# A hand-written slot order for a gated attention and feed-forward block: values with keys, queries and outputs in other places, and output rows carried over the slot's end

## The reference

```
def reference(x, ctx, g_xattn, g_ffn, Wq, Wkv, Wout, w_gate_up, w_down):
    q = layernorm(x) @ Wq.T                       # 16 heads of 32
    k, v = split(ctx @ Wkv.T)
    s = where(causal, q_h @ k_h.T / sqrt(32), lowest)
    o = softmax(s) @ v_h                          # per head, then joined
    x = x + tanh(g_xattn) * (o @ Wout.T)
    xq = quant(layernorm(x)); w1 = quant(w_gate_up)
    gate, up = split(xq @ w1.T)                   # 1408 each
    h = quant(silu(gate) * up)
    return x + tanh(g_ffn) * (h @ quant(w_down).T)
```

## Time and profile before

| | us |
|---|---|
| median of 3 runs (lowest, highest) | 743.07 (741.93, 746.26) |
| the profiled execution's own time | 743.81 |
| its span, first to last instruction | 742.0 |
| mean granted clock of PE, of full speed | 0.989 |
| PE, DVE, POOL, ACT busy | 705.7, 608.5, 570.9, 418.4 |

### The profile page before, as it was taken

One profiled execution on the slowest core, in us unless ns is written; L12 is line 12 of the kernel. 1 busy time (PEld: TensorE's weight loads), 2 busy tenths in 40 slices (PEclk: granted clock), 3 DMA queues, 4 the chain that ended last, 5 costly groups with the idle time before them and its releaser, 6 DMA issues.

```text
span 742.0 us, 17026 instructions
## 1 busy us (share of the span) xinstructions
PE 705.7 (95%) x5335; PEld 510.3 (69%) x5360; DVE 608.5 (82%) x1900; ACT 418.4 (56%) x658; POOL 570.9 (77%) x763
## 2 busy tenths in 40 slices
PE   3979999999999999999999998999999999999995
PEld 2868888889878888888888886565444444444442
DVE  5576878888888887787788887769999999999994
ACT  5457658668567567577576565265444344343441
POOL 6438768787787787787787877469888988888883
PEclk9989999999999999999999999999999999999998
DMA  8795977877886887877778759934566675565656
GB/s 250 186 247 158 253 159 220 238 178 210 219 209 192 231 199 210 208 212 211 190 217 226 189 139 236 271 102 121 87 163 143 145 165 132 144 154 129 159 124 193
DMA packets 137983, 137.59 MB, mean 185 GB/s; under 512 B 90381, under 2 KB 99879, under 8 KB 137767
## 3 DMA queue, kind: packets, MB, share of 16 engines
q1 hardware_dynamic: 136832, 135.97, 72.4%
q10 hardware_dynamic: 1063, 0.54, 0.4%
HBM read 40.24 MB, written 25.31 MB: 88 GB/s over the span
## 4 chain that ended last, share of the span: by engine, by line
PE 86%; DVE 4%; SPq 3%; DMA 3%; issue 2%; ACT 2%; POOL 1%; ACTq 1%; DVEq 0%; POOLq 0%
PE psum L2036 19%; PE psum L1642 12%; PE psum L1666 11%; PE psum L1708 10%; PE psum L2046 9%; PE psum L1595 5%; PE psum L1682 5%; PE psum L1654 3%; PE psum L1593 3%; PE psum L1629 3%; SPq L271 2%; PE psum L1684 2%; PE psum L1579 2%; DVE hmax L1503 1%; DMA heads<-nmT 1%
## 5 line engine op out<-in xcount | busy, mean ns | idle before, releaser
L1226 DVE CUSTOM_DVE_ANT_0 junk<-psum,mask 128x128 f32<-128x128 f32 (+1 forms) x512 | 152.3, 353 | 42.2 <-PE psum L1595 41.6
L2036 PE MATMUL psum<-w1q,xqb 128*128 128x512 bf16 (+1 forms) x753 | 158.3, 363 | 1.1 <-issue 0.3
L615 POOL TENSOR_SCALAR_AFFINE_SELECT prob<-prob 128x512 f32<-128x512 f32 x128 | 85.3, 666 | 71.1 <-ACT prob L924 69.7
L924 ACT ACTIVATE prob<-psum 128x768 f32<-128x768 f32 x128 | 103.7, 810 | 60.9 <-PE psum L1684 58.8
L798 POOL TENSOR_TENSOR hidden<-hidden 128x512 f32<-128x512 f32 (+1 forms) x94 | 110.8, 1194 | 29.4 <-ACT hidden L1141 29.3
L2036 PEld LDWEIGHTS psum<-w1q,xqb 128*128 128x128 bf16 x768 | 74.3, 98 | 80.2 <-issue 3.0
L1146 ACT ACTIVATE hidden<-hidden,round_bias,hinv 128x1408 f32<-128x1408 f32 x31 | 48.4, 1560 | 103.4 <-DVE hinv L1513 103.4
L623 POOL TENSOR_TENSOR prob<-prob 128x256 f32<-128x256 f32 x128 | 94.3, 743 | 6.2
L2046 PE MATMUL psum<-w2q,hqT 128*128 128x512 bf16 x331 | 79.0, 386 | 6.0 <-DMA hqT<-hq 5.4
L1642 PE MATMUL psum<-xT_hi,wq_hi 128*128 128x256 f32 x256 | 75.7, 296 | 0.5 <-POOL xT_lo L630 0.4
L1595 PE MATMUL psum<-heads 96*128 96x256 f32 x256 | 75.1, 335 | 0.0
(11 more groups left out here) (127 smaller groups left out, 1780.7 us busy)
## 6 DMA issues: line engine op xcount, KB each, us to landing
heads<-k_hi SPq DMA_DIRECT2D x128, 128.0 KB, 3.9
heads<-q_hi SPq DMA_DIRECT2D x128, 128.0 KB, 4.2
xln<-x_dram SPq DMA_DIRECT2D x16, 512.0 KB, 4.6
heads<-k_lo SPq DMA_DIRECT2D x64, 128.0 KB, 4.3
heads<-q_lo SPq DMA_DIRECT2D x64, 128.0 KB, 2.8
x<-x_dram SPq DMA_DIRECT2D x16, 512.0 KB, 4.6
x_scratch<-x SPq DMA_DIRECT2D x16, 512.0 KB, 4.8
x1b<-x_scratch SPq DMA_DIRECT2D x32, 256.0 KB, 3.4
```

What stands on the lines that cost most here:

```text
L615: pool.affine_select(out=blk, in_=blk, compare_op=ALU.is_ge, fill=0.0, base=0, pattern=[[0, 4], [1, P]], channel_multiplier=-1).then_inc(s ...
L924: act.activation(prob[:, g % 2, pair % 2, 0:CAUSAL // P].rearrange("p k h q -> p h k q"), psum[:, 2:4, 0:CAUSAL].rearrange("p h (k q) -> p ...
L1226: dve.tensor_tensor_reduce(junk[:, n % 2, 0:w], psum[:, h % 2, cols], m, 1.0, LOWEST, ALU.add, ALU.max, mx[:, X % 2, t, h:h + 1]).then_inc ...
L2036: last = pe.matmul(psum[:, bank, 0:w], xqb[:, t % 4, k, :], w1q[:, k, half * I + o:half * I + o + w], start=(k == 0), stop=(k == KH - 1))
```

## The change

All five engines' lists are written in another order, in the slots, the opening and the ending. The calls are the same but for `spare`, 12 matmuls where there were 15, and a few waits that belong to the order. In a slot of PE:

- `values(b+1, 0)` and `values(b+1, 1)` stand together early in the slot; before, the first was done a slot ahead.
- the four `queries` of batch b+2 stand in one slot, between the `keys` and to the end; before, the first two were done a slot ahead.
- `transposed(b+3, 0)` stands at the end and its second tile at the start of the next slot.
- `output(b-1, ...)`: three of four calls close the slot, and `output(b-2, 1, 1)` opens the next.

The core of the diff (SP's, DVE's and PE's slots; POOL's, ACT's, the opening and the ending are rewritten in the same manner):

```
-        WORK = [("V", 1, 1, 6), ("Q", 1, 2, 6), ("K", 0, 2, 7), ("K", 1, 2, 6), ("O", 0, -1, 7), ("T", 0, 3, 6),
+        WORK = [("T", 1, 2, 6), ("V", 0, 1, 6), ("V", 1, 1, 7), ("Q", 0, 2, 6), ("K", 0, 2, 7), ("K", 1, 2, 7),
...
                 def slot(b):                 # SP
-                    spread_k_lo(b + 1, 2)
+                    load_rows(b + 3)
+                    spread_q_lo(b + 1, 2)
                     spread_k_lo(b + 1, 3)
+                    spread_k_hi(b + 1, 2)
+                    move_weights(b + 1)
+                    spread_k_hi(b + 1, 3)
+                    store_xq(b - 3)
+                    load_weights(b + 2)
+                    spread_q_hi(b + 1, 2)
                     store_x1(b - 2)
...
+                    load_residual(b - 1)
...
+                    spread_q_hi(b + 2, 0)
...
                 def opening():               # DVE
-                    ones(0)
                     measure_x(0)
+                    ones(1)
...
+                    low_weights(2, wo_hi, wo_lo, wo_raw)
+                    ones(0)
+                    maxima(0, 0)
...
                 def opening():               # ACT
...
                     copy_k(0, 0)
+                    weights(0)
                     copy_k(0, 1)
...
                 def ending():                # PE
...
                     pe.wait_ge(s["v_copied"], 2 * (B - 1) + 2)
                     output(B - 3, 1, 0)
-                    weigh(B - 2, 3)
+                    score_pair(B - 1, 0)
                     output(B - 3, 1, 1)
-                    pe.wait_ge(s["u_copied"], GROUPS * (B - 2) + 4)
-                    gate_up(0, 0, 0, 4)
...
                 def values(X, t):
-                        if X == 0:
-                            pe.wait_ge(s["split"], 1)
```

More of the change, by code:

```diff
@@ L1381, in ending @@
                     normalise(B - 3, 1)
-                    for h in range(0, 5):
+                    for h in range(0, 3):
+                        maxima(B - 1, h)
+                    residual(B - 4, 1)
+                    for h in range(3, 7):
                         maxima(B - 1, h)
                     low_o(B - 3, 0)
-                    for h in range(5, 10):
+                    for h in range(7, 11):
                         maxima(B - 1, h)
-                    low_o(B - 3, 1)
-                    maxima(B - 1, 10)
@@ L1389, in ending @@
-                    maxima(B - 1, 11)
-                    step(B - 4, 0)
-                    for h in range(12, 16):
+                    measure(B - 4, 0)
+                    for h in range(11, 16):
                         maxima(B - 1, h)
                     negate(B - 1)
+                    measure(B - 4, 1)
+                    low_o(B - 3, 1)
+                    step(B - 4, 0)
+                    reciprocals(B - 2)
+                    split_reciprocals(B - 2)
                     step(B - 4, 1)
+                    normalise(B - 2, 0)
@@ L1768, in opening @@
                     scores(0, 15)
[L1769 to L1771 removed]
                     pe.wait_ge(s["t_copied"], 6)
                     values(1, 0)
[L1774 to L1775 removed]
+                    maxima_rows(0)
+                    pe.wait_ge(s["t_copied"], 5)
+                    values(1, 1)
                     scores(1, 0)
@@ L1837, in slot @@
                     score_pair(b, 2)
-                    keys(b + 2, 0)
+                    queries(b + 2, 0)
                     scores(b + 1, 4)
@@ L1862, in slot @@
                     score_pair(b, 7)
-                    output(b - 1, 1, 0)
-                    maxima_rows(b + 1)
-                    output(b - 1, 1, 1)
-                    weigh(b, 2)
-                    queries(b + 3, 0)
-                    weigh(b, 3)
-                    values(b + 2, 0)
-                    queries(b + 3, 1)
+                    queries(b + 2, 3)
+                    maxima_rows(b + 1)
+                    weigh(b, 2)
+                    output(b - 1, 0, 0)
+                    transposed(b + 3, 0)
+                    weigh(b, 3)
+                    output(b - 1, 0, 1)
+                    output(b - 1, 1, 0)
                 def ending():
```

719 lines of the change are left out of this document (346 added, 373 removed).

## The result

| | before | changed |
|---|---|---|
| median (lowest, highest), us | 743.05 (741.93, 746.26) | 774.70 (772.33, 788.97) |
| ratio, 95% interval | | 1.041 (1.038 to 1.044) |
| span of the profiled execution, us | 742.0 | 774.1 |
| mean granted clock | 0.989 | 0.977 |

It is 4.1% slower; 739.0 had been forecast. The highest of the four changed runs, 788.97, had a lower granted clock (0.961) than the other three and is left out of the ratio. The windows of the changed kernel, which answer to the earlier trace rows: the twelve full slots 1 to 12 (first pair of batch 1 to first pair of batch 13), everything behind them, and three stretches at the halved clock.

What follows compares the result with a forecast made beforehand. PE was taken as the bound, the only engine full in the slots. Slots -2.6, opening -3.0 and ending +1.5 sum to -4.1, giving 739.0 us against the median of 743.07; range 733.5 to 748.

Steps and rivals of the forecast that it cites:

- The queue, taken as no wait: SP's queue ahead of scores(b+1, 8): third quarter's high part of the queries lands 0.4 us before it is wanted.
- The bound of 5.2: Upper end of the 2.3 to 5.2 us taken for the landing of the third quarter's last piece.
- the burst of 2.5 MB within 8 us: Load on SP's queue in a slot, named as the argument for the rival that queries wait there.
- the rule that the prediction cited: Each DMA engine consumes descriptors in ring order, so the third quarter lands behind the rows and weights issued ahead of it.
- The rival of the queue wait: Queries wait on SP's queue at scores(b+1, 8), 0.65 us a slot, at most 1.3; time 747.4; chance 0.2.
- DVE at the slot's end: Inverted sums and residual ready 8.7 and 9.4 us behind the last score, margins 1.1 and 0.9: no wait on PE.
- The joints, -0.2 a slot: Fewer gaps between PE's calls shorten each slot to 28.5 us, -2.6 us over 13 slots, bounds 0 and -5.
- The opening, -3: Up to slot 1's start: earlier key pieces -1, less POOL work -2; -3 us in all, from -5 to +1.5.
- like-for-like start: Slot 1's start before the change, 81.50, set to 77.4 for the calls that leave the opening.
- the two costs named against the gain: Opening: ACT's weights piece ahead of a copy; DVE's low part of Wo (2.3) and memset (3.5) ahead of the first maximum.
- The ending, +1.5: Batch 15's first pair waits longer for its maxima and a w1 load comes later: +1.5 us, from -2 to +5.
- Its mark: Sign for the ending term: the first pair of batch 15 with more than 2 us of waiting.

Runs made afterwards that it cites:

- Experiments 2: Changed kernel with the third quarter's high part of the queries issued two places earlier on SP, ahead of the xq store and weights load: 757.4 us, ratio 1.019.
- experiment 3: Changed kernel, order kept, each w1 piece load in slots 2 to 12 bringing 16 of 128 rows (output wrong): 763.4 us, ratio 1.027.
- experiment 9: On top of 6, the next batch's query high parts go ahead of the keys' low parts on SP: 747.7 us, ratio 1.0052.
- experiment 1: Changed kernel with the third quarter's high part of the queries issued first in SP's slot, ahead of the rows' load: 759.4 us, ratio 1.021.
- 5: On top of experiment 1, maxima_rows(b+1) moved behind weigh(b, 2) on PE: 759.3 us, ratio 1.019.
- 6: On top of experiment 1, POOL's low_k(b+2, 1) moved behind the last mask and sum of the slot: 752.9 us, ratio 1.011.
- 7: Changed kernel with POOL's low_k(b+2, 1) moved behind the slot's last mask and sum, SP's order kept: 784.2 us, ratio 1.051.
- experiment 11: Kernel before with one POOL call moved: the seventh pair's sum ahead of the low part of the second tile's transposed rows: 752.2 us, ratio 1.012.
- experiment 10: On top of experiment 9, low part of Wo and one memset put back behind batch 0's maxima on DVE: 752.0 us, ratio 1.011.
- experiment 4: On top of experiment 1, batch 0's queries issued ahead of rows 2, context 2 and weights 1 in SP's opening: 760.7 us, ratio 1.024.

## Why the prediction was wrong

**The queue, taken as no wait.** This is the step that failed: "With 4.1 for the landing (the burst is long, but 3.5 is the median) and 1.1 for the store it is 11.3, 0.4 before it is wanted. I take no wait." Measured in slot 5: the piece lands 13.1 behind the load's issue, where 11 or so had been said. SP took the 7.0 that the forecast's terms give for it; all of the error is the landing, 6.1 for 4.1 (5.8 on average). The bound of 5.2 was no bound but one slot's highest; the same view of the kernel before, from 111 to 425 us, has 6.0:

```profile
DMA to landing us min/median/max: 2.2/4.0/6.0
```

The forecast had the number in hand ("the burst of 2.5 MB within 8 us") and did not divide it. From the load to the third quarter 2560 KB are issued; at the 208 GB/s of the earlier trace rows they need 12.6 us, against the 11.2 that PE gave them behind the load's issue (211.36 to 222.57, where the scores would start without a wait). That would have said 1.4 us of wait, in every slot. That it comes so close is in part luck. The 208 is a mean over a slot in which the DMA engines are busy for 0.79 of the time; in the burst itself they move more:

```profile
211.36:224.45 13.09, 11.38 (x98) 10.04 (x96) 10.55 (x45) 7.70 (x13) 11.90 (x19) 1.00 0.91 271
```

At 271 GB/s 2560 KB need 9.7 us, and no wait would have been said. But 13.09 us at 271 GB/s are 3.5 MB: some 0.9 MB that are issued behind the piece (a store of 512 KB is the next, 0.6 us later) were moved before it landed. In the twelve slots it was 3.1 to 3.5 MB at 248 to 271 GB/s. So the landing was made of the bytes ahead and of a share of those behind. Experiments 2 and 3 show that bytes decide: at an unchanged place 448 KB less land it 1.8 us earlier in slot 5 and 2.5 on average.

On the rule that the prediction cited: the Trainium skill, page "DMA: Bandwidth & Descriptors", section "Queues, rings and completion order", also says that completion is not in the order of issue. This trace agrees with both halves: the third quarter landed late behind the backlog ahead of it, yet its second piece landed at 224.44, behind the first piece of the fourth quarter, which was issued 1.3 later and landed at 224.16.

**The rival of the queue wait** named the place, the mechanism and the sign, and had a chance of 0.2. Its price, 0.65 a slot and at most 1.3, was three times too small: 1.95 a slot (23.4 in twelve). And it left out the clock: three waits halved it, another 7.4 us.

**DVE at the slot's end.** The forecast took the negation at 0.4 from the kernel before and concluded "Margins of 1.1 and 0.9: no wait" for the inverted sums. These margins held: no wait for `rec` in slots 2 to 12. But the maxima's rows, which wait for the negation, got no margin at all in the working, though the order gave them only a pair and a query call of cover. The change put POOL's low part of keys on top of the negation. In the changed kernel PE's longer wait hid this; it would have cost 1.07 a slot by itself. The Trainium skill, page "SBUF — State Buffer", section "SBUF: two separate sides", names two kinds of DVE instruction that exclude GpSimd: those with two SBUF inputs, against a GpSimd instruction that reads SBUF, and those in a two-port mode. The prediction applied the first kind alone, and in the opening alone. Here the one-input negation was held like the two-input one (0.90 and 0.56 for 0.18 and 0.19); in which mode it ran, no trace shows.

**The joints, -0.2 a slot.** In experiment 9 nine of slots 2 to 12 are 28.68 long, from broadcast to broadcast, against 28.70 before: the term is a tenth of what was said. (The mean of the eleven is 28.70, since two of them are 28.84 and 28.76.) 0.05 to 0.09 a joint was read from single gaps, and the new order's transposes (0.53) and maxima's rows (0.31 for 0.14) have larger ones that were not counted.

**The opening, -3.** The like-for-like start was 77.4. Eight profiles have the changed kernel's opening, call for call. Their starts of slot 1, and how long the clock had been halved until then:

| | changed | 1 | 2 | 3 | 5 | 6 | 7 | 9 |
|---|---|---|---|---|---|---|---|---|
| slot 1 starts | 80.9 | 80.0 | 76.6 | 82.0 | 77.9 | 79.0 | 81.2 | 77.3 |
| halved for, us | 17.1 | 20.5 | 6.8 | 20.5 | 13.7 | 17.1 | 20.5 | 6.8 |

The mean is 79.4, so the opening lost 2.0 where it was to gain 3. With the clock halved as long as before (6.8 us), it is 0.1 to 0.8 ahead. The start goes with the time at the halved clock, which differs between executions of one opening by 14 us; no term of the sum spoke of it, and which wait makes it fall I have not taken apart. That the clock is the cause is not shown either: the old opening stood at 81.5 after 6.8 us of it, and in experiment 11 at 81.8 after 13.7. Of the two costs named against the gain and not priced, experiment 10 says that DVE's order is none; ACT's, a piece of weights ahead of a copy, no run tests. SP's order for the queries of batch 0 is cleared by experiment 4. One more difference is in the traces and not tested: the first negation of batch 0 takes 1.07 us beside POOL in the changed kernel (at 52.22), 0.56 before (at 45.97).

**Slot 1**, in no term, takes 31.3 in experiment 9, where 28.7 less its absent output call would be 27.2. The broadcast stands ahead of everything else and waits 1.1 for the inverted sums; in a steady slot two output calls, 2.9 us, stand between the last weighing and it, in the opening none. The remaining 3 us, a clock halved from 81.2 to 84.6 and pairs that wait for ACT, I have read and not tested.

**The ending, +1.5.** Its mark, more than 2 us of waiting, came in kind and not in size: the first pair of batch 15 waits for the maxima, by this row, and PE loses 1.8 (3.2 had been said).

```profile
512.18 0.39 PE L1676 MATMUL psum<-heads 98*128 98x256 f32 x1 [1.63 <-DMA heads<-nmT]
```

As a whole the sign is the other: from slot 13 on, the same eight profiles take 318.4 on average; before and experiment 11 take 314.4, and 5.6 us of calls have moved in (two query calls 2.9, values 0.8, transposes 0.4, an output 1.5). That is 1.6 gained, within the spread of either group (316 to 321, 313 to 316), and so not shown.

## What to carry to other kernels

When transfers are moved behind others, sum the bytes from the head of the burst to the piece that is waited for, and some of what is issued right behind it (here 2.6 MB, and 0.5 to 0.9 more), and divide by the rate within a burst (here 248 to 271 GB/s), not by the mean of a slot; the highest landing time of one quiet slot is not a bound. A wait that is found is not all there is: give every wait of the new order a margin, for removing one here showed the next three times over, and a fix of the lower one alone gave nothing. Follow POOL's list against DVE's short instructions that PE waits for: the place of one call on POOL was worth 1% of this kernel.

## What the runs showed of the hardware

- A DVE instruction that takes 0.18 us took up to 1.10 while POOL ran an instruction on SBUF, and ended within 0.05 us of POOL's; the two-input one of 0.19 took 0.56. In experiment 1 this happened in slots 2 to 12 without exception; maxima read from PSUM kept their 0.42 in the same stretches.
- The landing of a 128 KB piece was 2.3 us on an empty queue (changed kernel, 227.05) and 6.1 behind 2.3 MB; in experiment 3 448 KB less were worth 1.8 us at an unchanged place in slot 5, and 2.5 on average. Transfers issued behind a piece moved before it had landed: 3.5 MB from the load to the landing in slot 5, of which 2.6 are the pieces up to it.
- Behind PE's waits of equal length the clock falls or does not: of three losses of 1.9 us in slots 3, 4 and 5 of the changed kernel, it was halved behind the first alone, for 3.4 us; behind 3.2 in slot 1 and 2.6 in slot 12 for 6.8 each, behind 2.6 in slot 8 not.
